# In the first attention, queries and turned maxima are added in a PSUM bank by TensorE and copied by ScalarE, in place of VectorE's addition

## The chip, the cores and the metric

The kernel runs on one core of a Trainium2 chip. The metric is the device time of one execution in microseconds (us). A core has five engines with instruction queues of their own: PE (TensorE, matrix products into the PSUM banks), DVE (VectorE), ACT (ScalarE), POOL (GpSimd) and SP (SyncE, which here only issues DMAs). They wait for each other through semaphores; each engine takes its instructions strictly in program order.

## The reference, cut to what matters

Eight samples of 128 tokens by 128 features go through four gated layers of cross-attention and feed-forward; the layers' attentions differ. The change touches the attention of layer 1 only:

```
q = split_heads(layernorm(x) @ wq.T + wq_b)          # 16 heads of 8
k, v = split_heads(ctx @ wk.T + wk_b), split_heads(ctx @ wv.T + wv_b)
scores = einsum('bhqd,bhkd->bhqk', q, k) / sqrt(8)
out = einsum('bhqk,bhkd->bhqd', softmax(scores, axis=-1), v)
x = x + tanh(g_xattn[1]) * (out @ dense.T + dense_b)
```

## The kernel before, in words

Layer 0 (a gated recurrence and a mixture of experts) comes first, then three attentions, a = 0, 1, 2, each with a "head" that projects queries, keys and values and a loop over the eight samples ("batches" b = 0 to 7). Between and behind them stand the feed-forward parts. The change is in the loop of a = 0, with n = 8a + b as the running number and u = b % 2 as the buffer.

Queries and keys lie transposed in f16, QU and KU: of each head's 32 rows, 24 hold the eight features three times (high and low parts), and the rows from 24 on are free for a bias; KU has the constant 1 there. For each batch:

- att_rows (PE, L1572): scores by query row into banks 0 and 1, in two halves p = 0, 1 of two head groups each.
- att_max (DVE, L1593): negated maxima of each row over the keys, four reductions, written into MB at column 24 of each 32.
- att_max_pe (PE, L1624): four transposes turn MB of the batch into bank 6 (f16, half the bank).
- att_max_dve (DVE, L1633): QX = bank 6 + QU, so QX holds the queries and, in row 24, the negated maximum.
- att_cols (PE, L1646): scores by key, less the maximum, into banks 2 and 3, two halves; the first waits for QX through a_qx.
- att_exp (ACT, L1664): four exponentials.
- att_pv (PE, L1683 and L1689): sums and weighted values into bank 4 or 5.
- att_norm (DVE, L1697 reciprocal, L1701 product), att_high (ACT, L1708), att_low (POOL, L1716), att_out (PE, L200, into bank 7), att_x (DVE, L1734, the residual), then the statistics of the next layer norm (DVE L343 and L349, POOL L353 to L359, L2016).

The order on each engine is written out by hand in att_pe, att_act, att_dve and att_pool; nothing is scheduled by a planner. Within iteration b the loop works on several batches: PE does column scores of b, row scores (second half) of b + 1, the last sums of b - 1, the second half of the column scores, the turning of the maxima of b + 1, the output product of b - 2, row scores (first half) of b + 2, and the first sums of b. DVE does the four maxima of b + 1, the normalisation of b - 1, QX of b + 1 and the residual of b - 2. ACT does the exponentials of b and att_high of b - 1. In iterations 1 to 6 POOL also converts tables for the third attention. At the loop's end DVE rounds the first half of the next feed-forward's input (L1960 to L1988) and PE turns it (L1995).

Before the loop, batch 0 goes through interleaved with the last three query projections (PE L200 in threes, ACT L1461, DVE L1468).

Of the kernel before, what the change touches and what calls it, by code (L numbers as in the profile page):

```python
# [8 lines left out]
NB, S, D = 8, 128, 128  # L9
# [28 lines left out]
def gated_mix_program(nc, t, out):  # L38
    fp32, fp16, bf16 = mybir.dt.float32, mybir.dt.float16, mybir.dt.bfloat16
    i32, u32 = mybir.dt.int32, mybir.dt.uint32  # L40
    ALU, ACT, AX = mybir.AluOpType, mybir.ActivationFunctionType, mybir.AxisListType.X

    ctx = ExitStack()
    with ctx:
        def sb(name, shape, dt=fp32):
            return ctx.enter_context(nc.sbuf_tensor(name, shape, dt))
# [3 lines left out]
        def sem(name):  # L50
            if name not in sems:
                sems[name] = ctx.enter_context(nc.semaphore(name))
            return sems[name]
# [22 lines left out]
        EYE, EYEH = sb("EYE", [128, 128]), sb("EYEH", [128, 128], fp16)  # L76
# [32 lines left out]
        MB = sb("MB", [128, 2, 4, 128], fp16)  # L109
        MF = sb("MF", [128, 3, NH])  # L110
        QX = sb("QX", [128, 2, 4, S], fp16)
# [16 lines left out]
        def bank(i, n=1):  # L128
            return PS[:, 512 * i:512 * (i + n)]
# [4 lines left out]
        def piece(at, n, dt=fp32, parts=128):  # L134

            view = SHARED[0:parts, at:at + (n if dt in (fp32, i32) else n // 2)]
            return view if dt == fp32 else view.bitcast(dt)
# [3 lines left out]
        KU, QU = (piece(at, 4 * TOK, fp16).rearrange("p (g b s) -> p g b s", g=4, b=NB) for at in (8192, 10240))  # L141
# [285 lines left out]
        def turn_one_act(act, j, b):  # L427
            act.wait_ge(sem("xt_turned"), NB * j + b + 1)
            act.activation(XH[:, b, :], bank(7)[:, 128:256], ACT.Copy).then_inc(sem("xt_high"), 1)
# [1183 lines left out]
        def att_max_pe(pe, a, b, u):  # L1613
            n = NB * a + b
            if a == 1:
                pe.wait_ge(sem("a_msplit"), 5 * b + 5)
            else:
                pe.wait_ge(sem("a_max"), 4 * n + 4)
            if n == 0:
                pe.wait_ge(sem("consts32"), 5)  # L1620
            else:
                pe.wait_ge(sem("a_qx"), n)
            for g in range(4):
                last = pe.transpose(bank(6).bitcast(fp16)[:, 128 * g:128 * g + 128], MB[:, u, g, :], EYEH[:])  # L1624
            last.then_inc(sem("a_mt"), 1)

        def att_max_dve(dve, a, b, u):

            n = NB * a + b
            dve.wait_ge(sem("a_mt"), n + 1)  # L1630
            if n >= 2:
                dve.wait_ge(sem("a_cols"), 4 * n - 4)
            dve.tensor_tensor(QX[:, u], bank(6).bitcast(fp16)[:, 0:512].rearrange("p (g s) -> p g s", g=4), QU[:, :, b, :], ALU.add)\  # L1633
                .then_inc(sem("a_qx"), 1)
# [23 lines left out]
        def att_exp(act, a, b, u, j):  # L1658

            n = NB * a + b  # L1660
            act.wait_ge(sem("a_cols"), 4 * n + j + 1)
            if n:
                act.wait_ge(sem("a_pv"), 4 * n + j - 3)
            act.activation(PF[:, j, :], bank(2 + j % 2), ACT.Exp).then_inc(sem("a_exp"), 1)  # L1664
# [38 lines left out]
        def att_high(act, a, b, u):  # L1703
            n = NB * a + b
            act.wait_ge(sem("a_norm"), n + 1)
            if n >= 2:
                act.wait_ge(sem("a_out"), n - 1)
            act.activation(ATH[:, u, :], AT[:, u, :], ACT.Copy).then_inc(sem("a_at_hi"), 1)  # L1708
# [31 lines left out]
        def att_pe(pe, a):  # L1740
# [6 lines left out]
            att_rows(pe, a, 0, 1)  # L1747
            proj_pe(pe, a, "q", 14)
            att_max_pe(pe, a, 0, 0)
            proj_pe(pe, a, "q", 15)  # L1750
            att_rows(pe, a, 1, 0)
            pe.wait_ge(sem("p_lo"), 16 * a + 14)
            for b in range(NB):
                u = b % 2
                if b == 1:
                    pe.wait_ge(sem("p_lo"), 16 * (a + 1))
                att_cols(pe, a, b, u, 0)
                if b + 1 < NB:
                    att_rows(pe, a, b + 1, 1)
                if b >= 1:  # L1760
                    att_pv(pe, a, b - 1, 1 - u, 2)
                    att_pv(pe, a, b - 1, 1 - u, 3)
                att_cols(pe, a, b, u, 1)
                if b + 1 < NB:
                    att_max_pe(pe, a, b + 1, 1 - u)
                if b >= 2:
                    att_out(pe, a, b - 2, u)
                if b + 2 < NB:
                    att_rows(pe, a, b + 2, 0)
                att_pv(pe, a, b, u, 0)  # L1770
                att_pv(pe, a, b, u, 1)
                if a == 0 and b == NB - 1:
                    quant_turn_pe(pe, 0)
                if j and b >= 3:
                    turn_one_pe(pe, a, j, k, b - 3)
# [14 lines left out]

        def att_act(act, a):
            k, j = NEXT[a]
            for b in range(NB):
                u = b % 2
                for i in range(4):
                    att_exp(act, a, b, u, i)
                if b >= 1:
                    att_high(act, a, b - 1, 1 - u)
                if a == 0 and b == NB - 1:
                    quant_act(act, 0)  # L1800
                if j and b >= 3:
                    turn_one_act(act, j, b - 3)
            att_high(act, a, NB - 1, 1)
            if j:
                for b in range(NB - 3, NB):
                    turn_one_act(act, j, b)

        def att_dve(dve, a):
# [14 lines left out]
            att_max_split(dve, a, 0, 0)  # L1823
            proj_dve(dve, a, 14)
            att_max_dve(dve, a, 0, 0)
            proj_dve(dve, a, 15)
            for b in range(NB):
                u, end = b % 2, b == NB - 1
                if not end:
                    att_max(dve, a, b + 1, 1 - u, 0)  # L1830
                    att_max(dve, a, b + 1, 1 - u, 1)
                if own and b >= 2:
                    att_low(dve, a, b - 2, u)
                if j and b >= 4:
                    turn_one_dve(dve, j, b - 4)
                if not end:
                    att_max(dve, a, b + 1, 1 - u, 2)
                    att_max(dve, a, b + 1, 1 - u, 3)
                    att_max_split(dve, a, b + 1, 1 - u)
                if a == 0 and end:  # L1840
                    quant_scale_dve(dve, 0)
                if b >= 1:
                    att_norm(dve, a, b - 1, 1 - u)
                if not end:
                    att_max_dve(dve, a, b + 1, 1 - u)
                if a == 0 and end:
                    quant_round_dve(dve, 0)
                if own and b >= 3:
                    ln_apply(dve, k, b - 3, b - 3, b - 3)
                if b >= 2:  # L1850
                    residual(b - 2)
                if a == 0 and b == NB - 2:
                    quant_max_dve(dve, 0)
# [144 lines left out]
        def quant_act(act, i):  # L1998
            act.wait_ge(sem("q_turned"), i + 1)
            act.activation(XQT[:, HF4[i], :].rearrange("p b s -> p (b s)"), bank(Q_TURN[i]).bitcast(fp16)[:, 0:512], ACT.Copy)\  # L2000
                .then_inc(sem("q_xt"), 1)
# [61 lines left out]
        @block.scalar  # L2063
        def _(act):
            act_loads(act)
            context_act(act)
            turn_act(act, 0)
            gates_act(act)
            mlstm_act(act)
            turn_act(act, 1)  # L2070
            moe_act(act, 0)
            head_act(act, 0)
            att_act(act, 0)
            head_act(act, 1)
            att_act(act, 1)
            route_act(act, 1)
            moe_act(act, 1)
            head_act(act, 2)
            att_act(act, 2)
            route_act(act, 2)  # L2080
            moe_act(act, 2)
# [154 lines left out]
```

## Time and profile before

| | |
|---|---|
| median of 3 runs | 704.96 us (703.7 to 705.64) |
| profiled execution | 705.0 us, span of the trace 703.2 us |
| PE busy | 608.2 us (86%) |
| DVE busy | 561.4 us (80%) |
| ACT busy | 365.5 us (52%) |
| POOL busy | 304.8 us (43%) |
| mean granted clock of TensorE | 0.949 |

The span is the time between the first and the last instruction of the trace; the rest of an execution's time lies around it. "Busy" is the time in which an engine had an instruction under way; matrix products overlap each other, so the start-to-start distance of two, and not the duration of one, is what each costs. The granted clock is 1.00 at TensorE's high level (2.4 GHz) and 0.50 at its low one (1.2 GHz). In a timeline "[0.49 <-PE PS L1572]" says that the engine sat idle for 0.49 us before the instruction, until that group of another engine released it.

### The profile page before, as it was taken

The numbers are of one execution on the slowest core, as the hardware profiler recorded it, in microseconds if no ns is written. First come the engines' busy times: TensorE is split into PE (matmuls) and PEld (weight loads), VectorE is DVE, ScalarE is ACT, GpSimd is POOL, SyncE is SP. The second block draws the span as 40 slices with busy tenths as digits, with TensorE's granted clock in tenths as the row PEclk, the third lists the DMA queues.
The fourth block names the chain that finished last, engine by engine and source line by source line (L and its number), as shares of the span: only waits on it lengthen the run. The fifth ranks groups of instructions, "written<-read, shape, count | busy, mean of one in ns | idle before, by whom it ended". The sixth has DMA issues, their size and how long they took to land.

```text
span 703.2 us, 16642 instructions
## 1 busy us (share of the span) xinstructions
PE 608.2 (86%) x5097; PEld 287.5 (41%) x5097; DVE 561.4 (80%) x1139; ACT 365.5 (52%) x669; POOL 304.8 (43%) x584
## 2 busy tenths in 40 slices
PE   3877899998688688998499999999999779993996
PEld 2432333444265433555244344344443334552443
DVE  6684887779788895787779899999999796765797
ACT  4663788985545352333345555555555464341553
POOL 2386577762037504667423334443344010235241
PEclk9996999999879899999899999999999999996899
DMA  8000111112300000000046666676566200000110
GB/s 291 12 1 16 34 42 48 46 43 50 90 3 3 1 0 3 1 2 3 11 133 177 166 170 173 171 181 166 165 174 173 73 1 2 2 3 13 39 52 32
DMA packets 43099, 48.66 MB, mean 69 GB/s; under 512 B 7916, under 2 KB 35896, under 8 KB 42920
## 3 DMA queue, kind: packets, MB, share of 16 engines
q1 hardware_dynamic: 42616, 47.26, 24.8%
q8 instruction: 32, 0.52, 0.3%
q10 hardware_dynamic: 432, 0.73, 0.3%
q14 instruction: 19, 0.16, 0.1%
HBM read 47.14 MB, written 0.82 MB: 68 GB/s over the span
## 4 chain that ended last, share of the span: by engine, by line
DVE 43%; PE 37%; ACT 8%; POOL 5%; issue 5%; DVEq 1%; DMA 1%; ACTq 0%; POOLq 0%
PE PS L200 25%; DVE SHARED L1186 9%; DVE PS L1036 8%; DVE PS L1049 4%; ACT SHARED L1016 4%; DVE SHARED L1468 3%; PE PS L1683 2%; PE PS L1689 2%; PE PS L1572 2%; DVE MF L1593 2%; DVE REC L1697 2%; DVE XN L359 2%; DVE MB L1593 2%; PE PS L1646 1%; DVE STAT L343 1%
## 5 line engine op out<-in xcount | busy, mean ns | idle before, releaser
L200 PE MATMUL PS<-XH,UH 128*128 128x512 f16 x296 | 115.3, 389 | 8.8 <-DVE PS L1036 3.1
L200 PE MATMUL PS<-SHARED,DNH 128*128 128x512 f16 x360 | 107.5, 380 | 8.8 <-DVE SHARED L1186 8.7
L200 PE MATMUL PS<-XL,UH 128*128 128x512 f16 x296 | 114.7, 388 | 0.0
L200 PE MATMUL PS<-XH,UL 128*128 128x512 f16 x296 | 114.4, 387 | 0.0
L918 POOL CAST DNH<-DF 128x128 f16<-128x128 f32 x90 | 32.3, 359 | 144.0 <-DMA DF<-in_down 99.4
L1016 ACT ACTIVATE SHARED<-PS 128x512 f16<-128x512 f32 x96 | 55.2, 597 | 75.3 <-DVE PS L1049 71.0
L1664 ACT ACTIVATE SHARED<-PS 128x512 f32<-128x512 f32 x96 | 52.1, 595 | 79.1 <-PE PS L200 58.6
L1186 DVE TENSOR_TENSOR SHARED<-SHARED 128x512 f16<-128x512 f32 x84 | 62.8, 754 | 21.3 <-ACT SHARED L1016 20.7
L1186 DVE TENSOR_TENSOR SHARED<-PS,SHARED 128x512 f16<-128x512 f32 x96 | 62.0, 686 | 8.9 <-ACT SHARED L1016 8.6
L200 PE MATMUL PS<-SHARED,DNL 128*128 128x512 f16 x180 | 68.5, 381 | 0.0
L985 ACT ACTIVATE SHARED<-PS 128x512 f32<-128x512 f32 x96 | 57.2, 597 | 16.8 <-PE PS L200 13.9
L1016 ACT ACTIVATE SHARED<-SHARED 128x512 f16<-128x512 f32 x84 | 52.9, 630 | 22.3 <-DVE SHARED L1028 17.4
L1049 DVE TENSOR_TENSOR PS<-PS,SHARED 128x512 f32<-128x512 f32 x92 | 59.7, 694 | 4.0
L1036 DVE TENSOR_TENSOR PS<-SHARED,PS 128x1024 f32<-128x1024 f32 x46 | 56.6, 1229 | 5.3 <-PE PS L200 0.6
L908 POOL TENSOR_TENSOR UL<-UF,UH 128x256 f16<-128x256 f32 (+1 forms) x90 | 56.7, 630 | 7.2
L200 PEld LDWEIGHTS PS<-SHARED,DNH 128*128 128x128 f16 x360 | 33.2, 98 | 56.9 <-issue 21.5
L200 PEld LDWEIGHTS PS<-XH,UH 128*128 128x128 f16 x296 | 29.1, 98 | 66.0 <-DVE PS L1036 26.2
L1668 POOL TENSOR_TENSOR SHARED<-SHARED,GPT 128x512 f32<-128x512 f32 x32 | 40.0, 1270 | 33.7 <-ACT SHARED L1664 33.7
L906 POOL CAST UH<-UF 128x256 f16<-128x256 f32 (+1 forms) x90 | 41.0, 455 | 30.0 <-PE PS L200 26.7
L1593 DVE TENSOR_REDUCE MB<-PS 128x4 f16<-128x512 f32 x64 | 41.2, 688 | 15.4 <-PE PS L200 11.0
L976 ACT ACTIVATE SHARED<-PS,B 128x512 f32<-128x512 f32 x64 | 43.4, 679 | 12.7 <-PE PS L200 10.0
L1461 ACT ACTIVATE SHARED<-PS,LOB,LOM 128x512 f16<-128x512 f32 x48 | 35.3, 777 | 28.3 <-PE PS L200 28.3
(284 smaller groups left out, 1193.1 us busy)
## 6 DMA issues: line engine op xcount, KB each, us to landing
SHARED<-w_rows_dram SPq DMA_DIRECT2D x31, 384.0 KB, 3.6
SHARED<-w_rows_dram SPq DMA_DIRECT2D x30, 256.0 KB, 3.9
UF<-in_up SPq DMA_DIRECT2D x58, 128.0 KB, 3.5
DF<-in_down SPq DMA_DIRECT2D x90, 64.0 KB, 2.7
SHARED<-w_rows_dram SPq DMA_DIRECT2D x31, 128.0 KB, 2.8
UF<-in_up SPq DMA_DIRECT2D x32, 64.0 KB, 1.8
SHARED<-t_values_dram SPq DMA_DIRECT2D x2, 1024.0 KB, 10.7
SHARED<-in_masks SPq DMA_DIRECT2D x1, 1024.0 KB
```

Source lines behind the costliest of these rows:

```text
L200: last = pe.matmul(dst, l, r, start=start and i == 0, stop=stop and i == len(pairs) - 1)
L906: pool.tensor_copy(UH[:, u, 0:n], UF[:, u, 0:n]).then_inc(sem("e_up_ready"), 1)
L908: pool.tensor_tensor(UL[:, u, 0:n], UF[:, u, 0:n], UH[:, u, 0:n], ALU.subtract)\
L976: act.activation(RH[u][:, hf, :], bank(hf), ACT.Relu, bias=B1[:, bass.ds(c, 1)]).then_inc(sem("e_act"), 1)
L985: act.activation(SG1[u][:, hf, :], bank(hf), ACT.Silu).then_inc(sem("e_act"), 1)
L1016: act.activation(HHI[:, u, hf, :], (bank(4 + hf), HF[:, hf, :])[m // 2] if m else RH[u][:, hf, :], ACT.Copy).then_inc(sem("e_high"), 1)
L1036: dve.tensor_tensor(dst, SG1[u].rearrange("p i n -> p (i n)"), bank(2, 2), ALU.mult).then_inc(sem("w1_gated"), 1)
L1049: dve.tensor_tensor(bank(4 + hf), bank(4 + hf), WB[u][:, HALF * hf:HALF * hf + HALF], ALU.mult)\
L1186: dve.tensor_tensor(HLO[:, u, hf, :], src, HHI[:, u, hf, :], ALU.subtract).then_inc(sem("e_low"), 1)
L1593: dve.tensor_reduce(dst, src, AX, ALU.max, negate=True).then_inc(sem("a_max"), 1)
L1664: act.activation(PF[:, j, :], bank(2 + j % 2), ACT.Exp).then_inc(sem("a_exp"), 1)
L1668: pool.tensor_tensor(PG[:, j, :].rearrange("p (g s) -> p g s", g=4), PF[:, j, :].rearrange("p (g s) -> p g s", g=4), over(GPT[:, b, :], 4) ...
```

## The change

In attention 0 alone, PE first multiplies the identity with the queries of the batch into bank 6 (128x512, f32, the whole bank) and then adds the four turned pieces of MB to it by plain products with the identity in place of transposes. ACT copies the bank into QX as f16; DVE's addition is gone. Attentions 1 and 2 keep the old way.

```
-            for g in range(4):
-                last = pe.transpose(bank(6).bitcast(fp16)[:, 128 * g:128 * g + 128], MB[:, u, g, :], EYEH[:])
+            if a:
+                for g in range(4):
+                    last = pe.transpose(bank(6).bitcast(fp16)[:, 128 * g:128 * g + 128], MB[:, u, g, :], EYEH[:])
+            else:
+                pe.matmul(bank(6), EYEH[:], QU[:, :, b, :], start=True, stop=False)
+                for g in range(4):
+                    last = pe.matmul(bank(6)[:, 128 * g:128 * g + 128], MB[:, u, g, :], EYEH[:], start=False, stop=g == 3)
             last.then_inc(sem("a_mt"), 1)
 
+        def att_max_act(act, a, b, u):
+
+            n = NB * a + b
+            act.wait_ge(sem("a_mt"), n + 1)
+            if n >= 2:
+                act.wait_ge(sem("a_cols"), 4 * n - 4)
+            act.activation(QX[:, u].rearrange("p g s -> p (g s)"), bank(6), ACT.Copy).then_inc(sem("a_qx"), 1)
+
         def att_max_dve(dve, a, b, u):
 
+            if a == 0:
+                return
...
         def att_act(act, a):
             k, j = NEXT[a]
+            if a == 0:
+                att_max_act(act, a, 0, 0)
             for b in range(NB):
                 u = b % 2
                 for i in range(4):
                     att_exp(act, a, b, u, i)
+                if a == 0 and b + 1 < NB:
+                    att_max_act(act, a, b + 1, 1 - u)
                 if b >= 1:
                     att_high(act, a, b - 1, 1 - u)
```

On ACT, from the end of the head's projections (L1461) into the loop; L1664 are the exponentials and L1708 is att_high. Before:

```order
L1461 ACTIVATE SHARED<-PS,LOB,LOM 128x512 x10
L1664 ACTIVATE SHARED<-PS 128x512 x8
L1708 ACTIVATE ATH<-AT 128x128
L1664 ACTIVATE SHARED<-PS 128x512 x4
L1708 ACTIVATE ATH<-AT 128x128
```

After, where line numbers are up to 19 higher (L1679 the exponentials, L1723 att_high, L1638 the new copy):

```order
L1461 ACTIVATE SHARED<-PS,LOB,LOM 128x512 x10
L1638 ACTIVATE QX<-PS 128x512
L1679 ACTIVATE SHARED<-PS 128x512 x4
L1638 ACTIVATE QX<-PS 128x512
L1679 ACTIVATE SHARED<-PS 128x512 x4
L1638 ACTIVATE QX<-PS 128x512
L1723 ACTIVATE ATH<-AT 128x128
L1679 ACTIVATE SHARED<-PS 128x512 x4
```

The copy of batch 0 stands behind the last projection; that of batch b + 1 stands behind the four exponentials of batch b and ahead of att_high.

On PE, from the last query projection but one through the turning for batch 1. Before:

```order
L1624 MATMUL PS<-EYEH,MB 128x128 x4
L200 MATMUL PS<-XH,WRH 128x512
L200 MATMUL PS<-XL,WRH 128x512
L200 MATMUL PS<-XH,WRL 128x512
L1572 MATMUL PS<-SHARED 128x128 x8
L1646 MATMUL PS<-QX,SHARED 128x128 x8
L1572 MATMUL PS<-SHARED 128x128 x8
L1646 MATMUL PS<-QX,SHARED 128x128 x8
L1624 MATMUL PS<-EYEH,MB 128x128 x4
L1572 MATMUL PS<-SHARED 128x128 x8
```

After (L1627 the new product, L1629 the four that add the turned maxima, L1661 the column scores):

```order
L1627 MATMUL PS<-SHARED,EYEH 128x512
L1629 MATMUL PS<-EYEH,MB 128x128 x4
L200 MATMUL PS<-XH,WRH 128x512
L200 MATMUL PS<-XL,WRH 128x512
L200 MATMUL PS<-XH,WRL 128x512
L1572 MATMUL PS<-SHARED 128x128 x8
L1661 MATMUL PS<-QX,SHARED 128x128 x8
L1572 MATMUL PS<-SHARED 128x128 x8
L1661 MATMUL PS<-QX,SHARED 128x128 x8
L1627 MATMUL PS<-SHARED,EYEH 128x512
L1629 MATMUL PS<-EYEH,MB 128x128 x4
L1572 MATMUL PS<-SHARED 128x128 x8
```

Each turning is one 128x512 product longer, and the product stands behind the wait for the maxima and ahead of what follows the turning.

On DVE, in the loop, from one batch's reciprocal to the next maxima. Before:

```order
L1697 RECIPROCAL REC<-PS 128x128
L1701 TENSOR_TENSOR AT<-PS,REC 128x128
L1633 TENSOR_TENSOR QX<-PS,SHARED 128x512
L1734 SCALAR_TENSOR_TENSOR X<-PS,G,X 128x128
L343 BN_STATS STAT<-X 128x6
L349 BN_AGGR MV<-STAT 128x2
L1593 TENSOR_REDUCE MB<-PS 128x4 x4
```

After:

```order
L1712 RECIPROCAL REC<-PS 128x128
L1716 TENSOR_TENSOR AT<-PS,REC 128x128
L1749 SCALAR_TENSOR_TENSOR X<-PS,G,X 128x128
L343 BN_STATS STAT<-X 128x6
L349 BN_AGGR MV<-STAT 128x2
L1593 TENSOR_REDUCE MB<-PS 128x4 x4
```

The addition is gone and nothing else has moved.

## Rows read from the trace of the kernel before

**Rows 1.** The chain of waits: share of the span by engine.
```profile
DVE 43%; PE 37%; ACT 8%; POOL 5%; issue 5%; DVEq 1%; DMA 1%; ACTq 0%; POOLq 0%
```
**Rows 2.** Busy time by stretch; us, busy (x instructions), clock, DMA share, GB/s.
```profile
184.50:188.00 3.50, 3.50 (x18) 1.33 (x18) 2.54 (x4) 0.78 (x1) 0.00 (x0) 0.51 0.00 0
...
191.40:198.20 6.80, 5.84 (x104) 4.08 (x98) 4.31 (x7) 2.17 (x4) 0.00 (x0) 0.50 0.01 2
198.20:208.40 10.20, 8.33 (x219) 6.09 (x216) 8.91 (x18) 5.00 (x11) 4.21 (x9) 1.00 0.01 2
208.40:211.80 3.40, 3.40 (x51) 2.52 (x53) 3.25 (x8) 1.30 (x3) 1.85 (x5) 0.50 0.02 5
211.80:232.20 20.40, 15.00 (x394) 11.00 (x392) 18.40 (x40) 9.89 (x20) 15.76 (x26) 1.00 0.01 3
232.20:235.60 3.40, 3.35 (x42) 2.40 (x43) 1.54 (x4) 0.60 (x1) 2.24 (x5) 0.52 0.00 0
```
**Rows 3.** Timeline of DVE in the loop: start us, us, instruction, idle before.
```profile
217.59 1.30 DVE L1593 TENSOR_REDUCE MB<-PS 128x4 f16<-128x512 f32 x2 [0.49 <-PE PS L1572]
...
219.99 0.41 DVE L1633 TENSOR_TENSOR QX<-PS,SHARED 128x512 f16<-128x512 f16 x1
220.32 0.34 DVE L1734 SCALAR_TENSOR_TENSOR X<-PS,G,X 128x128 f32<-128x128 f32 x1
...
221.12 1.26 DVE L1593 TENSOR_REDUCE MB<-PS 128x4 f16<-128x512 f32 x2
```
**Rows 4.** Timeline of PE in the loop, last row from attention 2.
```profile
218.95 0.40 PE L1624 MATMUL PS<-EYEH,MB 128*128 128x128 f16 x4
...
219.51 0.21 PE L200 MATMUL PS<-BL,SELE 4*128 4x128 f16 x1
...
220.89 0.40 PE L1646 MATMUL PS<-QX,SHARED 32*128 32x128 f16 x8
222.44 0.40 PE L1572 MATMUL PS<-SHARED 24*128 24x128 f16 x8 [1.15 <-DVE MB L1593]
...
582.26 1.04 PE L200 MATMUL PS<-SHARED,FLIP 128*128 128x512 f16 x4
```
**Rows 5.** Timelines of ACT and POOL, the loop and a copy behind it.
```profile
218.93 1.09 ACT L1664 ACTIVATE SHARED<-PS 128x512 f32<-128x512 f32 x2 [1.80 <-PE PS L1646]
220.10 0.31 ACT L1708 ACTIVATE ATH<-AT 128x128 f16<-128x128 f32 x1
...
244.84 0.60 ACT L410 ACTIVATE XH<-PS 128x512 f16<-128x512 f32 x1 [2.41 <-PE PS L404]
...
223.59 0.43 POOL L1716 TENSOR_TENSOR ATL<-AT,ATH 128x128 f16<-128x128 f32 x1
```
**Rows 6.** Timelines of PE, ACT and DVE, batches 0 and 1.
```profile
186.89 0.63 PE L200 MATMUL PS<-XH,WRH 128*128 128x512 f16 x1
187.32 0.63 PE L200 MATMUL PS<-XL,WRH 128*128 128x512 f16 x1
...
191.08 0.40 PE L1572 MATMUL PS<-SHARED 24*128 24x128 f16 x8 [2.10 <-DVE MB L1593]
...
192.87 0.61 PE L1624 MATMUL PS<-EYEH,MB 128*128 128x128 f16 x4 [0.96 <-DVE MB L1593]
...
188.26 0.78 ACT L1461 ACTIVATE SHARED<-PS,LOB,LOM 128x512 f16<-128x512 f32 x1 [0.94 <-PE PS L200]
...
198.38 0.96 DVE L1697 RECIPROCAL REC<-PS 128x128 f32<-128x128 f32 x1 [0.51 <-PE PS L1689]
```
**Rows 7.** Timeline of PE, the turn of the loop at the low clock.
```profile
208.32 0.56 PE L1624 MATMUL PS<-EYEH,MB 128*128 128x128 f16 x4
...
213.66 0.40 PE L1624 MATMUL PS<-EYEH,MB 128*128 128x128 f16 x4
```
**Rows 8.** Timelines of PE and DVE, the loop's tail.
```profile
232.25 0.60 PE L1995 MATMUL PS<-EYEH,SHARED 128*128 128x128 f16 x4 [1.34 <-DVE SHARED L1988]
...
234.79 0.96 DVE L1697 RECIPROCAL REC<-PS 128x128 f32<-128x128 f32 x1 [1.79 <-PE PS L1689]
```

## The prediction

> **What bounds the kernel now.** The chain of waits first: over the whole span DVE holds 43% of it and PE 37% [rows 1]. The first attention runs from about 184 to 238 us, so I read that stretch by engine. The table by stage [rows 2] shows DVE busy 18.40 of 20.40 us between 211.80 and 232.20, PE 15.00, ACT 9.89. The timelines then show one turn of the loop over batches, which repeats six times, from turning to turning of the maxima on PE every 5.29 us (218.95 - 213.66) [rows 4, 7]. DVE [rows 3]: two reductions (like those at 221.12), a wait of 0.49 us for PE's row scores, two more reductions at 217.59, a reciprocal and a product, the addition QX (L1633) at 219.99, the residual at 220.32, two small statistics, the next reductions at 221.12. DVE has nothing else to wait for. PE [rows 4] turns the maxima at 218.95, ends the output product at 219.51 + 0.22 = 219.73, starts the column scores at 220.89, then idles 1.15 us before the row scores at 222.44, released by DVE's maxima. So DVE is the bound of the loop, and one operation on it costs its start-to-start distance, not its 0.41 us: for QX 220.32 - 219.99 = 0.33 us.
>
> **The change, part by part.** Times of the loop below are in the frame of the run before.
>
> DVE loses eight additions. Those of batches 2 to 7 stand in the loop behind the product and ahead of reductions or the residual: 6 x 0.33 = -1.98 us. What could be late in their place: the residual (L1734) waits for PE's output product. PE now has one more 128x512 product ahead of it; such products follow each other at 0.22 us at the high clock ((1.04 - 0.38) / 3 in [rows 4], 0.38 being one alone) and at 0.43 at the low one (187.32 - 186.89, [rows 6]). The output product then ends at 219.95, and DVE could start the residual at 219.99 at the earliest. Just covered; bounds per turn are 0.11 (0.33 less the whole 0.22) and 0.41 (the duration). I take 0.33. The additions of batches 0 and 1 stand in front of waits (ACT's L1461, PE's row scores) and give nothing.
>
> PE gains eight 128x512 products (L1627), each ahead of four 128x128 ones that take the place of the transposes, at their price. For batches 2 to 7 the extra 0.22 us lies between the wait for the fourth maximum and the row scores of two batches on; PE's idle 1.15 us [rows 4] covers it even when the turn shortens by 0.33 (1.15 - 0.33 - 0.22 = 0.60 left). For batches 0 and 1 there is no such cover. Batch 0: the product comes before the last projection, on the chain to ACT's L1461 at 188.26; the clock is at its low level and rises near 188 [rows 2, 6], so of 0.43 us about half stays, 0.22. Batch 1: at 192.87, low clock, 0.43 whole, and PE is back to back from there until past DVE's reciprocal at 198.38. That makes 0.65 us of PE work. The low level ended at 198.20; if it ends there again, work pushed past that point runs at twice the rate, and 0.65 becomes 0.33. Bounds +0.33 and +0.65; I take +0.33.
>
> ACT gains eight copies. The trace has ACT copying 128x512 from f32 PSUM to f16 in 0.60 us [rows 5]. In the loop the copy stands behind the four exponentials. The last two run 218.93 to 220.02, so QX would be written by 220.62; PE asks for it at 220.89 + 0.22 = 221.11. Hidden with 0.49 us to spare, though QX comes 0.22 later than DVE's 220.40. Behind it on ACT stands the copy L1708 at 220.10, moved to about 220.6; its reader is POOL's subtraction, which takes the ATH of that turn at 223.59 [rows 5]: hidden. Batch 0: the copy queues behind ACT's last projection (188.26 + 0.22 + 0.78 = 189.26), so the first column scores come near 189.9, inside PE's idle 2.10 us before 191.08, which begins about 189 and was released by DVE's maxima [rows 6]: nothing. Batch 1: turned by about 194.2, copied by 194.8, and PE has a batch's first sums to do between the turning and the column scores: nothing.
>
> The Trainium skill says under "ScalarE: Activation LUTs", Rules for kernel authors, that additions and the like belong on VectorE and not on ScalarE. It speaks against this change. By the durations of this trace it is right about the operation itself (0.60 against 0.41 us) and would charge 0.19 a batch if the copy stood on the path; the rows above say that it doesn't.
>
> **The clock.** In the loop PE's clock fell to its low level (1.2 GHz, granted 0.50) from 208.40 to 211.80 and stood at its high one (2.4 GHz, granted 1.00) on both sides, so in one turn of six [rows 2]. In that turn PE was as late as DVE: from the turning at 208.32 to the next at 213.66, 5.34 us, 0.05 more than the next turn [rows 4, 7]. After the change PE does more and idles less, so I expect no fall there: -0.05. Were it to stay, PE would set that turn: 5.34 + 0.43 = 5.77 in place of 5.29 - 0.33 = 4.96, a loss of 0.81.
> At the tail the low level covered 232.20 to 235.60 [rows 2, 8], with PE's turning and sums on the chain until DVE's reciprocal at 234.79, for which DVE idled 1.79 us. All this now comes some 1.6 us earlier and the low stretch need not move with it. At the high level PE's 2.54 us there (232.25 to 234.79) would be 1.27 less; with a low stretch that lasts up to 1.6 us further into the projections, half of that time is lost, 0.8. Between -1.27 and +0.8 I take the row as it stands, +0.1 for the earlier start of the low stretch.
>
> **Sum.** +0.33 - 1.98 - 0.05 + 0.1 = -1.6 us. The next stages follow from DVE's residuals, and no transfer stands on the path there, so the shift is carried to the end. The profiled execution took 705.0 us (span 703.2), the median of the three runs is 704.96, so both give 703.4. With the terms at their bounds: 6 x 0.41 and the clock's best give 705.0 + 0.33 - 2.46 - 0.05 - 1.27 = 701.5; 0.65, 6 x 0.11 and the clock's worst (+0.8) give 705.8.
>
> **The rivals.**
> - *Another wait takes QX's place (no change).* The residual waits for the output product, and each turn keeps 0.11: 705.0 + 0.33 - 0.66 + 0.1 = 704.8. For it: only 0.04 us between 219.95 and 219.99, and a low clock in any turn breaks it. Against: a late residual is not yet late reductions; these need the row scores, which PE has by about 220.2.
> - *The clock gives more.* The tail's turning and sums run at the high level, or the low stretch before 198.20 ends sooner: 703.4 - 1.3 = 702.1, or any point between. For it: PE is denser. Against: in the tail PE waits for DVE and is idle just before. The Trainium skill ("TensorE: Matmul & The Clock Gate", Part 1) says that the throttled state is the default and activity releases it, which favours this case. Here PE was at work at the low level all through 191.40 to 198.20 [rows 2], so by the trace more work need not bring the rise forward.
> - *PE at its low clock becomes the bound (slower).* Each turn of the loop that runs low takes 5.77 us, PE's path from turning to turning with 0.43 more on it, against the 5.29 of before and the forecast's 4.96. Two such turns eat the gain (1.62 of 1.6); from there on it is slower. If all six turns ran low: 703.4 + 6 x 0.81 = 708.3. For it: one turn in six ran low before. Against: PE's idle in each turn shrinks.
> - *The copy becomes the wait (slower).* If ACT's copy ends after PE reaches the column scores, the addition has only moved along the path: 0.60 for 0.33, six times, +1.62 and +0.33 at the start, 706.9. It decides once the copy comes 0.49 us later than worked out, which needs exponentials that start later, as with a low clock in the loop.
>
> **How the numbers follow.** Chances: forecast 0.50 (its own range 702.8 to 704.3), another wait 0.18, more from the clock 0.20, low clock in the loop 0.07, copy as the wait 0.05. The three runs of before spread over 1.9 us, and 0.3%, 2.1 us, is about what a measurement of this kernel can tell from no change: faster means under 702.9, slower over 707.1. Faster: the clock case nearly whole and a tenth or two of the forecast, 0.28. Slower: the last two cases in part, 0.08. Same: 0.64. The range 702.0 to 705.5 leaves out the far end of the clock case and most of the two slower ones, under 2 in 10.
>
> **What would show it.** Right: reductions in DVE's loop start every 4.96 us; DVE goes from the product to the residual without a gap; the idle before PE's row scores is near 0.6; ACT's copies end before PE asks; reciprocal of batch 0 at about 198.7. Wrong: a gap on DVE before the residual released by PE (first rival); idle on PE before the column scores released by ACT (last rival); granted clock 0.5 in more than one turn between 200 and 230. If the whole is under 702.5, the tail's 232 to 235 stretch must have run at the high clock.

## The result, and the profile after

The changed kernel took 700.2 us (median of 4 runs, 700.14 to 700.27), the kernel before 705.11 us beside it (703.7 to 705.64): a ratio of 0.9934, 95% interval 0.9916 to 0.9951. That is 4.9 us faster, where 1.6 were forecast, and it lies below the range. The profiled execution took 700.27 us with a span of 698.5.

The loop of the first attention went as forecast. DVE of the changed kernel, one turn (columns as in [rows 3]):

```profile
216.63 0.95 DVE L1712 RECIPROCAL REC<-PS 128x128 f32<-128x128 f32 x1
217.61 0.29 DVE L1716 TENSOR_TENSOR AT<-PS,REC 128x128 f32<-128x128 f32 x1
217.82 0.34 DVE L1749 SCALAR_TENSOR_TENSOR X<-PS,G,X 128x128 f32<-128x128 f32 x1
...
218.62 1.26 DVE L1593 TENSOR_REDUCE MB<-PS 128x4 f16<-128x512 f32 x2
220.37 1.29 DVE L1593 TENSOR_REDUCE MB<-PS 128x4 f16<-128x512 f32 x2 [0.49 <-PE PS L1572]
221.58 0.95 DVE L1712 RECIPROCAL REC<-PS 128x128 f32<-128x128 f32 x1
```

From reciprocal to reciprocal it is 4.95 us. The residual follows the product with no gap: nothing took QX's place. PE of the same turn, against [rows 4]:

```profile
216.78 0.39 PE L1627 MATMUL PS<-SHARED,EYEH 128*128 128x512 f16 x1
217.00 0.39 PE L1629 MATMUL PS<-EYEH,MB 128*128 128x128 f16 x4
...
217.56 0.21 PE L200 MATMUL PS<-BL,SELE 4*128 4x128 f16 x1
...
218.94 0.40 PE L1661 MATMUL PS<-QX,SHARED 32*128 32x128 f16 x8
219.94 0.40 PE L1572 MATMUL PS<-SHARED 24*128 24x128 f16 x8 [0.61 <-DVE MB L1593]
```

The new product costs 0.22 us start to start, and PE's idle time went from 1.15 to 0.61 us. ACT, against [rows 5]:

```profile
216.76 1.08 ACT L1679 ACTIVATE SHARED<-PS 128x512 f32<-128x512 f32 x2 [1.26 <-PE PS L1661]
217.74 0.60 ACT L1638 ACTIVATE QX<-PS 128x512 f16<-128x512 f32 x1
218.21 0.32 ACT L1723 ACTIVATE ATH<-AT 128x128 f16<-128x128 f32 x1
```

The copy ends at 218.34, PE asks for it at 218.94: 0.60 us to spare. At the start of the loop, batches 0 and 1 on PE and DVE, against [rows 6]:

```profile
185.52 0.39 PE L1627 MATMUL PS<-SHARED,EYEH 128*128 128x512 f16 x1 [0.70 <-DVE MB L1593]
...
188.88 0.61 PE L1661 MATMUL PS<-QX,SHARED 32*128 32x128 f16 x8 [0.91 <-ACT QX L1638]
190.29 0.60 PE L1572 MATMUL PS<-SHARED 24*128 24x128 f16 x8 [0.80 <-DVE MB L1593]
...
192.29 0.61 PE L1627 MATMUL PS<-SHARED,EYEH 128*128 128x512 f16 x1 [0.96 <-DVE MB L1593]
```

```profile
197.63 0.95 DVE L1712 RECIPROCAL REC<-PS 128x128 f32<-128x128 f32 x1
```

PE does wait 0.91 us for ACT's first copy and then still waits 0.80 us for DVE's maxima: hidden, as worked out. The clock by stretch, against [rows 2]:

```profile
186.00:196.20 10.20, 7.52 (x99) 4.32 (x96) 4.96 (x8) 4.04 (x7) 1.59 (x2) 0.50 0.00 0
196.20:240.60 44.40, 35.62 (x780) 24.35 (x776) 39.19 (x95) 24.02 (x48) 28.67 (x52) 1.00 0.01 3
240.60:247.40 6.80, 6.28 (x23) 2.92 (x23) 6.76 (x23) 3.19 (x5) 0.44 (x2) 0.50 0.00 0
...
368.69:551.35 182.66, 175.64 (x781) 72.56 (x779) 167.81 (x222) 103.66 (x174) 75.34 (x172) 1.00 0.63 171
```

No turn of the loop ran low, and the tail ran high until 240.60; the low stretch then came behind it. The last row is the register loop of feed-forward 1, which answers to this row of the kernel before:

```profile
370.87:555.42 184.55, 175.67 (x780) 72.54 (x778) 167.98 (x222) 101.91 (x174) 75.12 (x172) 1.00 0.64 169
```

There the changed kernel is 1.89 us faster, over the same instructions at the same clock, far from any line of the change. It is the piece that the prediction had not seen. In two profiled executions the same point of DVE's stream can be compared all along:

| stretch, to | before, us | after, us | gained |
|---|---|---|---|
| last branch of feed-forward 0 on DVE | 162.15 | 161.31 | 0.84 |
| reciprocal of batch 0 | 198.38 | 197.63 | -0.09 |
| reciprocal of batch 6 | 228.56 | 225.73 | 2.08 |
| reciprocal of batch 7 | 234.79 | 230.90 | 1.06 |
| first reciprocal of attention 1 | 281.81 | 279.30 | -1.38 |
| register loop entered | 370.87 | 368.69 | -0.33 |
| register loop left | 555.42 | 551.35 | 1.89 |
| end of the span | 703.22 | 698.49 | 0.66 |

The first row lies ahead of the change: over the same instructions the two executions differ there, and the one before has one more stretch at the low level (17.26 to 20.68 us). In the rows with 1.06, -1.38, -0.33 and 0.66 the low stretches fell elsewhere in the two traces as well. So of the 4.73 us between the two spans, 3.88 are the start, the six turns and the register loop, and 0.85 is the net of the five other rows. For the last row the other profiles bear this out: from the end of the register loop to DVE's next branch the fourteen profiles take 113.6 to 113.9 us where no low stretch begins within 4 us of the loop's end, 115.1 to 115.3 where one does, and 115.6 to 115.9 where a second follows it, as in the kernel before (556.57 and 566.81; the changed kernel has one, at 551.20).

### The profile page after: what moved, and what is told of

It reads as the page before. It is cut to its first block, busy times and chain, and to the rows that moved or that the text cites. A ratio compares the mean times of both kernels' runs of the same rounds, so it can differ in the third digit from the quotient of the medians.

```text
span 698.5 us, 16658 instructions
## 1 busy us (share of the span) xinstructions
PE 603.9 (86%) x5105; PEld 285.1 (41%) x5105; DVE 558.4 (80%) x1131; ACT 370.7 (53%) x677; POOL 305.9 (44%) x584
## 4 chain that ended last, share of the span: by engine, by line
DVE 43%; PE 36%; ACT 8%; POOL 6%; issue 5%; DMA 1%; DVEq 0%; ACTq 0%; POOLq 0%
PE PS L200 24%; DVE SHARED L1186 9%; DVE PS L1036 8%; ACT SHARED L1016 4%; DVE PS L1049 4%; DVE SHARED L1468 3%; PE PS L1698 2%; DVE MB L1593 2%; DVE REC L1712 2%; DVE MF L1593 2%; PE PS L1572 2%; PE PS L1704 2%; DVE XN L359 2%; ACT SHARED L976 1%; DVE STAT L343 1%
## 5 line engine op out<-in xcount | busy, mean ns | idle before, releaser
L1016 ACT ACTIVATE SHARED<-PS 128x512 f16<-128x512 f32 x96 | 57.1, 597 | 68.5 <-DVE PS L1049 64.9
L1679 ACT ACTIVATE SHARED<-PS 128x512 f32<-128x512 f32 x96 | 52.1, 594 | 73.5 <-PE PS L200 58.5
L985 ACT ACTIVATE SHARED<-PS 128x512 f32<-128x512 f32 x96 | 57.2, 597 | 19.7 <-PE PS L200 14.4
L1016 ACT ACTIVATE SHARED<-SHARED 128x512 f16<-128x512 f32 x84 | 52.9, 630 | 21.8 <-DVE SHARED L1028 16.9
L200 PEld LDWEIGHTS PS<-XH,UH 128*128 128x128 f16 x296 | 29.1, 98 | 64.2 <-DVE PS L1036 23.8
L1461 ACT ACTIVATE SHARED<-PS,LOB,LOM 128x512 f16<-128x512 f32 x48 | 35.4, 776 | 28.7 <-PE PS L200 28.7
```

The lines of the kernel that those rows point to most:

```text
L200: last = pe.matmul(dst, l, r, start=start and i == 0, stop=stop and i == len(pairs) - 1)
L985: act.activation(SG1[u][:, hf, :], bank(hf), ACT.Silu).then_inc(sem("e_act"), 1)
L1016: act.activation(HHI[:, u, hf, :], (bank(4 + hf), HF[:, hf, :])[m // 2] if m else RH[u][:, hf, :], ACT.Copy).then_inc(sem("e_high"), 1)
```

## The experiments

**The register loop.** Feed-forward 1 is a loop in registers of 22 passes, two chunks of weights in each. On DVE, one pass of the kernel before and one of the kernel after:

```profile
441.67 1.29 DVE L1186 TENSOR_TENSOR SHARED<-PS,SHARED 128x512 f16<-128x512 f32 x2 [0.16 <-ACT SHARED L1016]
...
445.86 1.29 DVE L1186 TENSOR_TENSOR SHARED<-PS,SHARED 128x512 f16<-128x512 f32 x2 [0.23 <-ACT SHARED L1016]
```

```profile
438.71 1.29 DVE L1186 TENSOR_TENSOR SHARED<-PS,SHARED 128x512 f16<-128x512 f32 x2 [0.15 <-ACT SHARED L1016]
...
442.81 1.29 DVE L1186 TENSOR_TENSOR SHARED<-PS,SHARED 128x512 f16<-128x512 f32 x2
```

DVE's wait for ACT's second L1016 is gone in the changed kernel. And on ACT, before and after:

```profile
445.23 1.11 ACT L1016 ACTIVATE SHARED<-PS 128x512 f16<-128x512 f32 x2 [1.60 <-DVE PS L1049]
446.59 1.24 ACT L985 ACTIVATE SHARED<-PS 128x512 f32<-128x512 f32 x2 [0.26 <-PE PS L200]
```

```profile
442.18 1.19 ACT L1016 ACTIVATE SHARED<-PS 128x512 f16<-128x512 f32 x2 [1.52 <-DVE PS L1049]
443.63 1.34 ACT L985 ACTIVATE SHARED<-PS 128x512 f32<-128x512 f32 x2 [0.26 <-PE PS L200]
```

A pair of ACTIVATEs is 1.19 us when both start on time. Before, the first of the pair L1016 starts 0.08 us late (idle 1.60 for 1.52, and the pair is 1.11); after, the late one is in the pair L985 (1.34 for 1.24), which DVE doesn't wait for. In the records of single instructions the L1016 starts 163 ns after its register instruction in every pass of before, and 80 ns after it in every pass of after; in after, an L985 starts 182 ns after its wait instead of 87. Counted from the pass's branch the late one is the 4th instruction ahead of it before and the 18th after, and the change puts 14 more instructions on ACT ahead of the loop: eight copies and six waits. So the theory was that the late start stays at one place of ACT's stream and the code moves over it.

Its test needs no change of the attention. Small ACTIVATEs into a scratch tile, 1, 11 or 14 of them, in the kernel before:

```
             att_act(act, 1)
+            for i in range(14):
+                act.activation(PADT[:, i:i + 1], G[:, 0:1], ACT.Copy)
             route_act(act, 1)
```

> The kernel before, with one ACTIVATE of 128x1 (a copy of a constant into a scratch cell) put on ACT between attention 1 and the routing of feed-forward 1; nothing else. Theory (the place of ACT's code): in the register loop of feed-forward 1 one instruction of each pass, always at the same place of ACT's stream, starts 0.083 us late; before, it is the ACTIVATE L1016 that DVE waits for, and after the change, with 14 more instructions ahead of the loop on ACT, it is one that nobody waits for. One instruction more moves the late start onto the register instruction ahead of L1016, whose start is hidden by its wait: passes of 8.31 us in place of 8.39, 22 of them, -1.8 us, so about 703.3 us. Rival (the change alters how the engines meet at the loop's entry, and the passes keep it): one tiny instruction 20 us earlier on an idle engine changes nothing, 705.1 us, passes of 8.39 us.

> The kernel before with eleven such ACTIVATEs at the same place. Theory (place of ACT's code): the late start falls on the other ACTIVATE L1016 of the pass, the one eleven instructions earlier, for which DVE waits as well: passes of 8.39 us, 705.1 us as before, though more was added than in the run with one. Rival (entry of the loop, or any added instruction helps): the same time as with one or fourteen.

> The kernel before with fourteen such ACTIVATEs at the same place, as many instructions as the change adds to ACT ahead of the loop. Theory (place of ACT's code): the late start falls on L985 as in the changed kernel, passes of 8.31 us, about 703.3 us, with the first attention as it was before. Rival (entry of the loop): 705.1 us.

And the changed kernel with three waits fewer:

```
             act.wait_ge(sem("a_mt"), n + 1)
-            if n >= 2:
+            if n >= 5:
                 act.wait_ge(sem("a_cols"), 4 * n - 4)
```

> The changed kernel without three of the six waits for a_cols ahead of ACT's copy (batches 2 to 4), which PE's order makes superfluous: three instructions fewer on ACT, work and order the same. Theory (place of ACT's code): the late start falls on an ACTIVATE L1016 again, passes of 8.39 us in place of 8.31, +1.8 us, so about 702.0 us. Rival (entry of the loop, or the attention itself gave all of it): 700.2 us.

Measured, against the kernel before on the same chip (704.12 us, 18 runs); a pass is the mean of 22 between DVE's branches in the profiled execution, and the last column counts ahead of the branch of a pass the ACTIVATE that starts 83 to 95 ns late:

| kernel | median, us | ratio (95%) | pass, us | late ACTIVATE |
|---|---|---|---|---|
| before | 704.12 | | 8.389 | 4th (L1016) |
| one more | 702.13 | 0.9965 (0.9946 to 0.9984) | 8.305 | none |
| eleven more | 704.47 | 1.0001 (0.999 to 1.0012) | 8.385 | 15th (L1016) |
| fourteen more | 701.52 | 0.9957 (0.9942 to 0.9971) | 8.305 | 18th (L985) |
| changed, three waits fewer | 700.82 | 0.9954 (0.9941 to 0.9968) | 8.381 | 15th (L1016) |
| changed | | | 8.303 | 18th (L985) |

The place and the pass came out as the theory said in all four; the rival (the engines' meeting at the entry) falls, since eleven instructions do nothing where one and fourteen do. What makes one instruction of each pass late is not shown, only that its place moves with the number of instructions ahead. DVE with eleven more waits for the other L1016 of the pass:

```profile
443.32 1.29 DVE L1187 TENSOR_TENSOR SHARED<-PS,SHARED 128x512 f16<-128x512 f32 x2 [0.24 <-ACT SHARED L1017]
...
447.42 1.29 DVE L1187 TENSOR_TENSOR SHARED<-PS,SHARED 128x512 f16<-128x512 f32 x2
```

The wait has moved from the second pair to the first and is as long. With three waits fewer it is the same:

```profile
441.80 1.29 DVE L1186 TENSOR_TENSOR SHARED<-PS,SHARED 128x512 f16<-128x512 f32 x2 [0.24 <-ACT SHARED L1016]
...
445.90 1.29 DVE L1186 TENSOR_TENSOR SHARED<-PS,SHARED 128x512 f16<-128x512 f32 x2
```

In the times, three waits fewer were expected to bring the changed kernel to about 702.0, 3.1 us under the kernel before, and gave 700.82, 3.3 us under it on this chip. The changed kernel itself was not run on this chip, so this group shows what the longer passes cost it in the passes and not in the time; for that see the last group.

**The attention.** Two edits of the changed kernel, one that fills the slot on DVE again, and one in which DVE copies in ACT's place:

```
             if a == 0:
+                if b:
+                    dve.wait_ge(sem("a_pad"), b)
+                dve.tensor_tensor(PADQ[:], QU[:, :, b, :], QU[:, :, b, :], ALU.add).then_inc(sem("a_pad"), 1)
                 return
```

```
+            if a == 0:
+                dve.tensor_copy(QX[:, u].rearrange("p g s -> p (g s)"), bank(6)).then_inc(sem("a_qx"), 1)
+                return
```

> The changed kernel with a DVE addition of 128x512 f16 (QU + QU into a scratch tile) at the place where DVE's addition of QX stood in attention 0, eight of them; PE's product and ACT's copy stay. Theory (the slot on DVE is the attention's gain): about 0.33 us more for each of six turns of the loop, +2.0 us against the changed kernel, with the start of the loop unchanged; turns of 5.28 us again. Rival (the gain in the attention comes from PE's work and its clock, or from an earlier QX): the same time as the changed kernel. Passes of the register loop stay at 8.31 us under both, since ACT's stream is that of the changed kernel.

> PE's half alone: in attention 0 PE adds queries and turned maxima in the bank, but DVE copies the bank to QX where its addition stood, and ACT's stream is that of the kernel before. Theory (DVE's slot): an f32 copy of 128x512 takes longer on DVE than the addition's 0.41 us, nearer 0.6, so the turns of the loop get longer, by about 0.2 us for six turns, +1.1 us, and PE's products at the start cost up to 0.3: 0.8 to 1.5 us above the kernel before; register loop 8.39 us a pass. Rival (a denser PE keeps the clock up, and that was the gain): faster than the kernel before by 1 us or more.

The third applies the change to batches 2 to 7 alone (`if a or b < 2:` on PE, `if a == 0 and b >= 2:` on DVE, ACT's copies from b = 2 on), beside the changed kernel again:

> The change for batches 2 to 7 alone; batches 0 and 1 keep the transposes and DVE's addition. Theory: the start of the loop is as before (no product of PE at the low clock), the six turns keep their 0.33 us each; twelve instructions more on ACT ahead of the loop put the late start on a register instruction, which its wait hides or nearly so, so passes of 8.31 us: 0 to 0.4 us under the changed kernel. Rival (PE's products for batches 0 and 1 cost nothing, or the clock decides): the same as the changed kernel within 0.3 us, either side.

> The changed kernel once more, beside the other runs of this group. Both theories: about 4.5 to 5 us under the kernel before on the same chip. Of it, by the theory so far, 1.8 to 2.0 come from the register loop of feed-forward 1 (passes of 8.31 us) and 2.0 to 2.9 from the first attention; the rest is the clock.

The table gives, from each profiled execution, the six turns from the reciprocal of batch 0 to that of batch 6, and the two stretches behind. The last two rows are from the group above, whose kernel before took 704.12 us:

| kernel | median, us (before: 703.72) | six turns | to batch 7 | to attention 1 |
|---|---|---|---|---|
| before | | 30.18 | 6.23 | 47.02 |
| changed | 700.63 | 28.12 | 5.16 | 48.35 |
| slot filled | 708.05 | 31.00 | 6.23 | 48.53 |
| DVE copies | 706.28 | 31.70 | 6.23 | 48.10 |
| batches 2 to 7 alone | 701.03 | 28.13 | 5.17 | 48.59 |
| fourteen more on ACT | 701.52 | 30.88 | 6.23 | 46.99 |
| changed, three waits fewer | 700.82 | 28.30 | 6.23 | 48.64 |

DVE in the kernel with the slot filled, and in that with DVE's copy:

```profile
214.36 0.41 DVE L1646 TENSOR_TENSOR PADQ<-SHARED 128x512 f16<-128x512 f16 x1
214.69 0.35 DVE L1753 SCALAR_TENSOR_TENSOR X<-PS,G,X 128x128 f32<-128x128 f32 x1
```

```profile
215.56 0.68 DVE L1647 CAST QX<-PS 128x512 f16<-128x512 f32 x1
216.16 0.34 DVE L1750 SCALAR_TENSOR_TENSOR X<-PS,G,X 128x128 f32<-128x128 f32 x1
```

An addition of no use gives back all of the 0.33 us a turn: its reciprocals are 5.28 us apart, against 4.95. Its last turn, from 223.74 to 229.09, took 5.35, where the kernel before took 4.48 (224.08 to 228.56). This 0.87 is no slot of 0.33: in that turn the addition took 1.28 us in place of 0.41.

```profile
224.93 1.28 DVE L1646 TENSOR_TENSOR PADQ<-SHARED 128x512 f16<-128x512 f16 x1
```

```profile
223.65 2.28 POOL L1965 TENSOR_TENSOR SHARED<-SHARED 128x512 f16<-128x512 f32 x2
```

The seven other additions took 0.41 or 0.42 us each, and POOL did nothing meanwhile; this one met the second of POOL's two operations, which ended at 225.93. DVE's addition of QX, which reads one operand from a PSUM bank, took 0.41 us at this place (225.27, in the kernel before) beside the same operation of POOL. Without this 0.87 the filled slot costs 2.0 us in six turns (31.00 - 28.12 - 0.87), as expected.

DVE's copy has a slot of 0.60, and its turns are 5.55 us. So the slot on DVE decides, and PE's products alone give nothing: that kernel is slower than before, 1.0049 (1.0019 to 1.008). By the medians it is 2.6 us slower, where 0.8 to 1.5 were expected; its six turns account for 1.5. The slot filled was expected 2.0 us above the changed kernel and took 708.05, 7.4 above it, ratio 1.0041 (1.0013 to 1.0068) to before, more than its profiled execution of 704.98; its nine runs lie between 702.26 and 709.25, and by their mean clocks TensorE was at the low level for 64 us in the fastest and 86 in the slowest, 78 on average, against 65 in the changed kernel beside it. So most of the excess goes with the clock; why this kernel met more of the low level is not shown.

The low level in the loop costs more than the one turn of the kernel before suggested. There the turn with the low stretch took 5.34 us; in the kernels with eleven and with fourteen more instructions, whose attention is the old one, the low stretch fell at another place of the turn, and that turn took 5.99 (218.58 to 224.57 with fourteen). That is why "fourteen more" has 30.88 in the table. Of the six profiles of the old attention, four have a low stretch that begins within the six turns; of the six of the new one, none has. Whether the change brings that about is not shown.

The tail depends on the clock. Where PE's turning and sums run at the high level, the stretch to batch 7 is 5.16 or 5.17 us; in the other rows of the table it is 6.23. The changed kernel with three waits fewer has the same instructions there as the changed one, and fell to the low level earlier:

```profile
229.80:236.60 6.80, 5.92 (x51) 3.40 (x52) 4.63 (x14) 1.68 (x3) 3.20 (x7) 0.50 0.00 0
```

The stretch to attention 1 takes 48.3 to 48.8 us in each of the six profiles of the new attention, whether its tail ran high or low, and 46.9 to 48.8 in those of the old one. So the 1.38 us lost there in the first pair is not simply the tail's gain given back. It goes with where the low stretches lay in the head; whether the new attention favours that is not shown.

For batches 2 to 7 alone the time is the changed kernel's, 0.9956 (0.9937 to 0.9975) beside 0.9946 (0.993 to 0.9961), and its median is 0.4 us above, where 0 to 0.4 below was expected. That does not make PE's two products at the start free: by their mean clocks its runs spent 71 us at the low level, those of the changed kernel 65. The traces compare them at like clock. In this kernel and in the changed one the low stretch lies at the same place (185.86 to 196.10 and 185.98 to 196.22), and from the row scores ahead of the first turning (L1572) to the reciprocal of batch 0 they take:

```profile
183.58:196.83 13.25, 9.69 (x148) 6.16 (x150) 9.15 (x15) 4.81 (x8) 1.59 (x2) 0.61 0.01 1
```

```profile
183.67:197.63 13.96, 10.45 (x152) 6.12 (x152) 8.29 (x14) 5.90 (x10) 1.59 (x2) 0.63 0.00 1
```

The kernel with one more instruction on ACT, whose attention is the old one, takes 13.25 us as well. The products cost 0.71 us here. Where the low level comes in two pieces, as in the kernel before (13.88 us) and another profile of the changed one (14.26), they cost 0.38.

ACT's late start falls on no ACTIVATE in the kernel for batches 2 to 7 alone, and the passes take 8.31 us, as expected. The changed kernel was expected 4.5 to 5 us under the kernel before on this chip and was 3.1 under it.

**Two by two, and one instruction far ahead.** On one chip:

> The changed kernel, for a table of two by two on one chip: the first attention old or new, the register loop's late start on an awaited instruction (8.39 us a pass) or not (8.31). This is new and 8.31. If the two effects simply add, it is as far under the kernel before as the next two runs of this group are together, about 4 us.

> The kernel before with fourteen small ACTIVATEs ahead of feed-forward 1: old attention, 8.31 us a pass. By the passes alone 1.8 to 1.9 us under the kernel before; the three-round run gave 2.6.

> The changed kernel with three waits fewer on ACT: new attention, 8.39 us a pass. By the turns of the attention alone 2.0 to 2.1 us under the kernel before, and as much as 3 if its tail or the stretch behind it runs at the high clock more often.

> The kernel before with one small ACTIVATE, now ahead of the head of attention 0, 180 us before the register loop instead of 20. Theory (the place of ACT's code, so only the count of instructions ahead of the loop matters): passes of 8.31 us as in the run with one at the later place. Rival (something near the loop, such as ACT arriving a little later there): 8.39 us, as in the kernel before.

| kernel | attention | pass, us | median, us | range | ratio (95%) |
|---|---|---|---|---|---|
| before | old | 8.389 | 704.38 | 702.99 to 707.35 | |
| fourteen more | old | 8.309 | 700.5 | 699.62 to 703.27 | 0.9942 (0.9923 to 0.9961) |
| changed, three waits fewer | new | 8.397 | 701.26 | 700.1 to 709.91 | 0.9956 (0.9941 to 0.9972) |
| changed | new | 8.309 | 700.83 | 699.84 to 703.24 | 0.9953 (0.9937 to 0.9969) |
| one more, 200 us ahead | old | 8.309 | 701.95 | 699.73 to 704.9 | 0.9961 (0.9943 to 0.9979) |

The pass of "before" is that of the first profile. The one instruction far ahead starts at 160.80 us, some 200 us ahead of the register loop and not 180; those of the other kernels start between 341 and 344, some 20 to 30 us ahead. It does there what it does nearby: the count of instructions ahead of the loop matters, and not when they run.

The expectation that the two effects add failed in the times. Alone they give 3.9 and 3.1 us, together 3.6. Each alone gives more than its stretch (1.8 to 1.9 in the loop, about 2.0 in the six turns, less what PE's products cost at the start). Part of this is the clock. From a run's span and mean granted clock follows an estimate of its time at the low level, (1 - clock) x 2 x span: on average 68.5 us before, 64.5 with fourteen more, 64.2 with three waits fewer, 67.6 in the changed kernel. Among the runs of one kernel on this chip (76 runs in all) 1 us more at the low level goes with about 0.27 us more time. At equal time at the low level, the estimate puts the three kernels 2.5, 1.2 and 3.1 us under the kernel before, each to some 0.3; without the one run of 709.91 us, 2.7, 1.6 and 3.2. The two alone then make 3.7 to 4.3 in place of 7.0, beside 3.1 to 3.2 together. This is an estimate from the spread of the runs and not a test: why the kernels met different amounts of the low level, these runs don't settle.

Where a low stretch falls decides its price. In the run of 709.91 us one lay from 352.6 to 362.8, in the chunks of feed-forward 1 ahead of its register loop, and from attention 1's first reciprocal to the register loop that execution took 94.2 us; the kernel with one more instruction, with a low stretch from 353.0 to 359.8, took 93.4; the twelve others, without one there, took 88.6 to 89.4.

## Why the prediction was wrong

- **The six turns** were -1.98 and -0.05, measured -2.08 (30.18 to 28.10 in the first two profiles). Right, with the slot of 0.33 and no turn at the low clock; the filled slot shows the cause.
- **PE's products at the start** were +0.33, with bounds of 0.33 and 0.65, and measured +0.09 in the pair of profiles. That is luck: the low stretches lay elsewhere (186.00 to 196.20, in place of 184.50 to 188.00 and 191.40 to 198.20). At like clock the products cost 0.38 and 0.71 us, so the term was as large as forecast or larger, and the upper bound a little too small. A reading beside it was off too: between 191.40 and 198.20 PE was busy for 5.84 of 6.80 us, not all through.
- **ACT's copies hidden**: right, with 0.60 us to spare where 0.49 were worked out, and the first one inside PE's wait.
- **The clock's two terms** were -0.05 and +0.1. The first had its size from one execution, in which the low stretch cost 0.05 us in its turn; in other profiles of the old attention it cost 0.7. For the second, the tail gave 1.06, within the bound of 1.27, and the stretch behind it took 1.38 more. So the rival that the clock gives more was seen in the tail, but not in the sum of the two stretches.
- **The step that failed is "the next stages follow from DVE's residuals, and no transfer stands on the path there, so the shift is carried to the end".** It asked what waits change behind the attention and found none, and so put all stages behind it at nothing. But the change alters the length of ACT's instruction stream, and the register loop of feed-forward 1 runs 8.303 us a pass in place of 8.389: 22 x 0.085 = 1.9 us, a term as large as the whole forecast. The kernels with one and with fourteen more instructions show it apart from the attention.
- With that term the sum is -1.6 - 1.9 = -3.5, about 701.5. On other chips the changed kernel was 3.1 and 3.6 us under the kernel before, so the sum so mended fits there; the 4.9 of the first comparison, of four runs each, is 1.3 more. In its profiled pair the net of the stretches in which only the low level moved is 0.85 us in favour of the changed kernel. What more there is in the medians is not shown.
- Of the rivals, no other wait took QX's place, PE at the low clock did not become the bound, and the copy did not become the wait. The Trainium skill's rule that additions belong on VectorE ("ScalarE: Activation LUTs", Rules for kernel authors) holds here for the operation's own time only in so far as the ACTIVATE took 0.60 us where DVE's addition took 0.41. The two are not the same operation: the same copy of the bank took DVE 0.68 us. And the rule doesn't tell where to put it when ACT waits and DVE doesn't.

## What to carry to other kernels

An operation on the engine that bounds a loop costs its start-to-start slot in each turn, and moving it to an engine with idle time pays even where it takes longer there, as long as the result is ready before it is asked for. A change of the number of instructions on an engine can move the time of a register loop hundreds of us away that it doesn't touch: compare such loops pass by pass before crediting a gain to the edit, and try a few idle instructions ahead of the loop as a control. Here one small ACTIVATE took 1.9 us out of the register loop, nearly as much as the rewrite of the addition took out of the six turns (2.1). And compare stretches at like clock: the cost of PE's two products at the start was 0.09 us in the first pair of profiles, and 0.71 where the low stretches lay alike.

## What the hardware showed unexpectedly

In this register loop one instruction of ACT in each pass starts 83 to 95 ns late, at a place of the engine's stream that stays, whichever instruction stands there: the 4th, 15th or 18th ahead of the branch as 0, 11 or 14 instructions are put ahead, and hidden where it falls on a register instruction that waits. It costs 0.08 us a pass if another engine waits for that instruction, and nothing otherwise. A DVE addition of 128x512 in f16 with both operands in SBUF took 1.28 us in place of 0.41 in the one turn in which POOL worked beside it. And the low stretches of TensorE's clock come at other moments in each execution: the thirteen other profiles passed the last branch of feed-forward 0 between 160.0 and 161.8 us, the kernel before at 162.15, though their instructions up to there are the same.
